# Four engines' written-out stage orders replaced in a fused four-layer kernel, loop and both ends

## The reference, cut to what matters

```python
# layer 0: attention (16 query heads, 1 key/value head, band mask), gate, RMS norm, minus the mean over tokens
attn = softmax(mask(q @ k.T * scale)) @ v @ Wo + bo
gate = silu(concat([attn, x]) @ Wg + bg)
out = rms(attn * gate + x * (1 - gate)) * w;  x = out - mean(out, over tokens)
# layer 1: each token attends to 3 context rows near its index, weights relu(score)^2 / sum
x = x + near_attention(rms(x), rms(ctx)) @ Wo
# layer 2: self attention, then cross attention, 16 heads of 64, layer norms, relative position bias
x = attention(ln(x), ln(x)) + x;  x = attention(ln(x), ln(ctx)) + x
# layer 3: a Mamba-2 block (4-tap causal conv, 8 heads, gated, RMS norm), then cross attention, 8 heads of 32
x = x + rms(scan(silu(conv(rms(x) @ Win))) * silu(z)) @ Wout
x = x + softmax(mask(ln(x) @ Wq @ k.T)) @ v @ Wo
```

## Time and profile before

| | |
|---|---|
| timed runs | 1283.28, 1285.97, 1286.2 us (median 1285.97) |
| span of the profiled execution | 1284.9 us (its only time on record), mean granted TensorE clock 0.985 |
| head: start to the loop's first stage | 237.93 us |
| loop: 11 turns | 809.48 us, 73.59 each |
| tail: last turn's end to the last instruction | 237.49 us |
| busy share of PE, DVE, ACT, POOL | 95%, 69%, 60%, 26% |

### The profile page before, as it was taken

The page is one execution under the profiler, slowest core; times in us unless marked ns, Lnnn a source line. Parts: engine busy times, 40 slices in busy tenths (PEclk is TensorE's granted clock), DMA queues, the critical chain, the costliest instruction groups (busy, mean ns, idle before and its releaser), DMA issues.

```text
span 1284.9 us, 27988 instructions
## 1 busy us (share of the span) xinstructions
PE 1225.8 (95%) x9644; PEld 988.3 (77%) x9644; DVE 883.1 (69%) x3414; ACT 770.2 (60%) x2658; POOL 332.6 (26%) x750
## 2 busy tenths in 40 slices
PE   5899899999999999999999999999999999999887
PEld 3568687788788787788788788878878787788665
DVE  4674667687686768678686867768676876836464
ACT  3447457565766756576775757576575655655533
POOL 2111441312314141222314131231414123112150
PEclk9899899999999999999999999999999999999899
DMA  7730001001010100001010100101010010000000
GB/s 219 290 120 13 34 2 43 13 11 44 0 49 4 49 4 25 28 8 45 0 49 4 44 9 8 45 0 49 4 49 4 16 37 34 5 6 1 9 1 13
DMA packets 28620, 44.67 MB, mean 35 GB/s; under 512 B 4716, under 2 KB 20620, under 8 KB 28056
## 3 DMA queue, kind: packets, MB, share of 16 engines
q1 hardware_dynamic: 26264, 31.42, 7.4%
q0 software_dynamic: 2304, 12.58, 2.7%
HBM read 37.64 MB, written 6.35 MB: 34 GB/s over the span
## 4 chain that ended last, share of the span: by engine, by line
PE 89%; DVE 5%; ACT 2%; issue 1%; DMA 1%; POOL 1%; SPq 0%; DVEq 0%; POOLq 0%
PE psum L574 57%; PE psum L568 11%; PE psum L759 5%; PE psum L782 4%; PE psum L625 3%; PE psum L821 2%; PE psum L876 1%; PE psum L836 1%; PE psum L647 1%; PE psum L916 1%; PE psum L677 1%; ACT A L938 1%; PE psum L891 1%; DVE A L1175 1%; ACT A L930 0%
## 5 line engine op out<-in xcount | busy, mean ns | idle before, releaser
L938 ACT ACTIVATE A<-A,small_ 128x128 f32<-128x128 f32 x640 | 248.5, 396 | 49.6 <-DVE small_ L1175 49.6
L930 ACT ACTIVATE A<-psum 128x512 f32<-128x512 f32 (+2 forms) x231 | 155.7, 700 | 173.7 <-PE psum L568 152.9
L568 PE MATMUL psum<-cst,A 128*128 128x128 f32 x888 | 131.5, 281 | 20.8 <-DVE A L1287 6.9
L568 PEld LDWEIGHTS psum<-cst,A 128*128 128x128 f32 x888 | 101.9, 143 | 43.8 <-issue 14.5
L938 ACT ACTIVATION_READ_ACCUMULATOR A<-A,small_ 128x1 f32 x640 | 125.0, 195 | 0.0
L1501 POOL TENSOR_SCALAR small_<-small_ 128x1 f32<-128x1 f32 x96 | 22.6, 236 | 370.1 <-DVE small_ L1189 203.7
L1175 DVE CUSTOM_DVE_ANT_0 A<-psum,cst 128x128 f32<-128x128 f32 x256 | 56.7, 287 | 66.6 <-PE psum L625 66.4
L1175 DVE CUSTOM_DVE_ANT_0 A<-psum,bias 128x128 f32<-128x128 f32 x264 | 58.4, 287 | 63.3 <-PE psum L759 63.3
L1185 DVE TENSOR_TENSOR A<-A,small_ 128x1024 f32<-128x1024 f32 x80 | 98.3, 1229 | 2.7
L938 ACT ACTIVATE sa_p<-sa_p,small_ 128x128 f32<-128x128 f32 x248 | 96.1, 398 | 4.3 <-DVE small_ L1175 4.3
L1366 DVE SCALAR_TENSOR_TENSOR A<-psum,half_cw,A 128x127 f32<-128x127 f32 (+2 forms) x270 | 70.7, 344 | 32.0 <-ACT A L1062 32.0
(11 more groups left out here) (314 smaller groups left out, 2886.8 us busy)
## 6 DMA issues: line engine op xcount, KB each, us to landing
kv_rows<-A SPq DMA_DIRECT2D x16, 256.0 KB
IN<-in_tokT SPq DMA_DIRECT2D x15, 256.0 KB, 2.6
A<-bias_rows SPq DMA_DIRECT2D x1, 2048.0 KB, 10.0
Wsakv<-in_wsa_kv SPq DMA_DIRECT2D x1, 2048.0 KB, 11.6
Wcakv<-in_wca_kv SPq DMA_DIRECT2D x1, 2048.0 KB, 12.8
ctx_end<-in_tokT SPq DMA_DIRECT2D x16, 128.0 KB, 2.2
out<-x_out SPq DMA_DIRECT2D x16, 128.0 KB, 1.7
IN<-in_ctx SPq DMA_DIRECT2D x15, 128.0 KB, 2.0
```

Source lines behind the costliest of these rows:

```text
L568: mm = pe.transpose(out[:, c * P:(c + 1) * P], src[:, c * P:(c + 1) * P], ident)
L930: return act.activation(out, in_, ACT.Copy)
L938: ins = act.activation(p[:, h * T:(h + 1) * T], p[:, h * T:(h + 1) * T], ACT.Exp, scale=-1.0, bias=sm(part, "nm", w * HU + h, w * HU + h + 1),
```

## The change

All twelve strings are replaced by other permutations (the same stages, each batch's part in the same inner order). In the loop, PE's `l0_s0`, `ca_v`, `ca_hat`, `ca_q`, `ca_s0` and both `sa_s` stages come earlier, `m_dtz`, `m_xbc`, `m_seg`, `m_heads`, `q3` later; between `m_xh` and `turn1` PE's new order is `l0_p1 sa_s0 l0_m1 m_heads kv1 attn0 sa_s1 ca_p0 gate0 ca_p1 m_sq m_out kv3 back0 ca_m hat3 sa_p0 center0 q3`, and DVE's from `m_xh` on is `m_xh sa_s0 m_heads ca_p1 attn0 m_sum sa_s1 sa_p0 m_sq gate0 m_out kv3 hat3 back0 sa_p1 center0 q3 turn1`. In the head, `o:bias_rows` and `o:l0_s0` come before `b:kv0` on PE; around batch 2's `near` stages (key `e`) `center0`, `turn1`, `near_q`, `sa_out` and `ca_out` come earlier than they did against `turn_o1`. At the tail's start `ca_q` moves ahead of `d:l0_m0`; at its end `h:hat3`, `h:c3_s`, DVE's `h:c3_p` and PE's `h:c3_out` each move ahead of the stage of batch 15 that they stood behind.

Two edits of code go with it. `m_tap` keeps its step marks per part (part 4 of two batches can now interleave): where another chained step of DVE came between two taps, the tap waits for all chained steps so far, otherwise per block as before. And the layer norm of the last attention gets small columns of its own, `r3` and `t3`.

```diff
@@ -117,25 +117,25 @@
 ORDER = {
-    "PE": "3132414314323141323412431112144432143421421312421414",
-    "Activation": "344341324314141323123114123142231422414",
-    "DVE": "21124134114443423134343142414442241214141112314",
-    "Pool": "4322411441112",
+    "PE": "3131324134343212314241214112313444134214142132421414",
+    "Activation": "334343142431124134211241313214213242414",
+    "DVE": "23121411431342443431424314224144412141411413124",
+    "Pool": "2124413144112",
 }
 
 
 HEAD = {
-    "PE": "obooobobooboooobobobobooooboooobooobeeabbeabaaebaebeaecdeddadacdaedacecdcdeccdecececdecegigfihfgifghgihgifighfgifiihfffihgifgffhgihiihfhifif",
...
-    "DVE": "oobooboobobbboooooooooobooooobooeaeabebbeaebbbeabddadaaddedacdeccecceceeeedecihifhgifiifhgffigfggfgffifhffifhhffihiifiiigihf",
...
+    "PE": "ooobobooooboooboobboobbbooooooboooobeebaebabaaeabebeaedeeddcadcadadacecdcdcecedececdccegegfifhigfighighgifghfihfiiigfffigfhfighfigihihfhifif",
...
+    "DVE": "oooboboobobbobooooooooobooooobooeaebaebbeaebbbeabddadaaddaceddeccecececedeecefhiihgfiiihffgfgfiggfffhfigfffihhfihfiifigiihif",
...
 }
 
 TAIL = {
-    "PE": "bdbadadbdabdcddddbdbacadbcdacdbacbdabacdbadacgaggagcfgacgfcafeifgfegfefgigfeieifieifeeeieeeifieieeihhjjhjhhjhjjhhhjjjhhjhjjhjhjhj",
...
-    "DVE": "cddbcadadddaaadbbadcabdbdaabdacddadaaccdggacagbaggcgfaegfefeeffegefieieeieeeeieieifeehijhjhhhjhjjhjhjhjhjhjhhjjjhhjjhjhj",
...
+    "PE": "bdbadadbabcdbddbdddadbacdcadcbdacadcbabddabagcagggcafgcagacffegfefgefigfgiefieifiefieeeieeeifieieeihhjjhjhhjhjjhhhjjhjhhjjjhjhhjj",
...
+    "DVE": "ddcadbcdaddabaadabdbcadbadbaadcadddaacdgcgaagcabggacefggeffeefeffegieieeieeeeieieiefehijhjhhhjhjjhjhjhhjhjhhjjhjjhjhjjhj",
...
 }
 
 
@@ -334,7 +334,7 @@
 
         _soft = [("nm", 2 * HU), ("sm", 2 * HU), ("rc", 2 * HU)]
         _norm = [("bn", 6), ("mv", 2), ("r", 1), ("r1", 1), ("ssq", 1), ("ssq1", 1), ("t1", 2)]
-        _mamba = [(n, HM) for n in ("dtp", "ab", "u", "den", "s", "sq", "po", "dt", "a")]
+        _mamba = [(n, HM) for n in ("dtp", "ab", "u", "den", "s", "sq", "po", "dt", "a")] + [("r3", 1), ("t3", 1)]
         _near = [("ms", 2), ("cr", 2), ("w", NEAR * H1), ("dn", H1)]
         small_places = {
             1: _soft + _norm + _near,
@@ -1351,7 +1351,7 @@
                 need(t, "m_thz")
                 dve.scalar_tensor_tensor(m.sz, m.thz, 1.0, m.Pd, ALU.add, ALU.mult).then_inc(sem["m_sz"], 1)
 
-            taken = [0] * CC
+            taken = {}
 
             def m_tap(d):
 
@@ -1359,17 +1359,23 @@
                     m = W4(t)
                     if d == 1:
                         need(t, "m_acc")
+                        taken[m.part] = [0] * CC, 0
+                    mine, reached = taken[m.part]
+                    beside = steps[0] == reached
+                    if d > 1 and not beside:
+                        after(steps[0])
                     for c in range(CC):
-                        if d > 1:
-                            after(taken[c])
+                        if d > 1 and beside:
+                            after(mine[c])
                         to = m.acc[:, c * T + d:(c + 1) * T]
                         ins = dve.scalar_tensor_tensor(to, m.P_4[:, c * T:(c + 1) * T - d],
                                                        half_cw[:, c * TAPS + TAPS - 1 - d:c * TAPS + TAPS - d],
                                                        to, ALU.mult, ALU.add)
                         if d < TAPS - 1:
-                            taken[c] = step(ins)
+                            mine[c] = step(ins)
                     if d == TAPS - 1:
                         ins.then_inc(sem["m_conv"], 1)
+                    taken[m.part] = mine, steps[0]
                 return run
 
             def m_silu(t):
@@ -1429,7 +1435,7 @@
             def normed3(t):
                 m = W4(t)
                 need(t, "c3_rstd")
-                normed(m.part, m.x5[:], m.hat3, sm(m.part, "r"), "c3_hat")
+                normed(m.part, m.x5[:], m.hat3, sm(m.part, "r3"), "c3_hat")
 
             def query3(t):
                 m = W4(t)
@@ -1495,9 +1501,9 @@
                 steps[0] += 1
                 pool.wait_ge(sem["pool_chain"], steps[0])
 
-            def rsqrt(part, out, src, scale, eps, name):
-
-                t = sm(part, "t1", 0, 1)
+            def rsqrt(part, out, src, scale, eps, name, at="t1"):
+
+                t = sm(part, at, 0, 1)
                 then(pool.tensor_scalar(t, src, scale, eps, ALU.mult, ALU.add))
                 pool.tensor_tensor(out, t, neg_half[:, 0:1], ALU.pow).then_inc(sem[name], 1)
 
@@ -1617,7 +1623,7 @@
             def deviation3(t):
                 m = W4(t)
                 need(t, "c3_var")
-                rsqrt(m.part, sm(m.part, "r"), sm(m.part, "mv", 1, 2), 1.0, 1e-5, "c3_rstd")
+                rsqrt(m.part, sm(m.part, "r3"), sm(m.part, "mv", 1, 2), 1.0, 1e-5, "c3_rstd", "t3")
 
             stages = {
                 "inputs": [ctx_rstd], "attn0": [near_rows], "gather": [gather], "back0": [rms0], "center0": [rms1],
```

More of the change, by code:

```diff
@@ L119 @@
 ORDER = {
-    "PE": "3132414314323141323412431112144432143421421312421414",
-    "Activation": "344341324314141323123114123142231422414",
-    "DVE": "21124134114443423134343142414442241214141112314",
-    "Pool": "4322411441112",
+    "PE": "3131324134343212314241214112313444134214142132421414",
+    "Activation": "334343142431124134211241313214213242414",
+    "DVE": "23121411431342443431424314224144412141411413124",
+    "Pool": "2124413144112",
 }
 HEAD = {
-    "PE": "obooobobooboooobobobobooooboooobooobeeabbeabaaebaebeaecdeddadacdaedacecdcdeccdecececdecegigfihfgifghgihgifighfgifiihfffihgifgffhgihiihfhifif",
-    "Activation": "oooboobobobobobbobobaeebaaebeedaecadadeacaddccededcceccdcefgfgifghgfiifhigfighgifihigfighhfhihfif",
-    "DVE": "oobooboobobbboooooooooobooooobooeaeabebbeaebbbeabddadaaddedacdeccecceceeeedecihifhgifiifhgffigfggfgffifhffifhhffihiifiiigihf",
-    "Pool": "oooboobobbaaebedadceeexdgfhifhffiiiih",
+    "PE": "ooobobooooboooboobboobbbooooooboooobeebaebabaaeabebeaedeeddcadcadadacecdcdcecedececdccegegfifhigfighighgifghfihfiiigfffigfhfighfigihihfhifif",
+    "Activation": "oooooboobobbbobbobobaebeaaebeeedaadcadeaacddcceddecccdeccegffgfhigfgiifhigfhigifihgifgihghfihhfif",
+    "DVE": "oooboboobobbobooooooooobooooobooeaebaebbeaebbbeabddadaaddaceddeccecececedeecefhiihgfiiihffgfgfiggfffhfigfffihhfihfiifigiihif",
+    "Pool": "obooooobbebaeabdadeecexdfihfifhgfiiih",
 }
 TAIL = {
-    "PE": "bdbadadbdabdcddddbdbacadbcdacdbacbdabacdbadacgaggagcfgacgfcafeifgfegfefgigfeieifieifeeeieeeifieieeihhjjhjhhjhjjhhhjjjhhjhjjhjhjhj",
-    "Activation": "baabadbdddaddbdadcabdcbacbdbcbdacgagcagcafgcfegfefigegefgfifeeiifeifeieiieiehhjhjjhjhhjjhjhjhjhjhj",
-    "DVE": "cddbcadadddaaadbbadcabdbdaabdacddadaaccdggacagbaggcgfaegfefeeffegefieieeieeeeieieifeehijhjhhhjhjjhjhjhjhjhjhhjjjhhjjhjhj",
-    "Pool": "cdabdacdddaagcegfegeeihjhjhjhj",
+    "PE": "bdbadadbabcdbddbdddadbacdcadcbdacadcbabddabagcagggcafgcagacffegfefgefigfgiefieifiefieeeieeeifieieeihhjjhjhhjhjjhhhjjhjhhjjjhjhhjj",
+    "Activation": "baabdabdbaddddcadadbbdcdacbcbdbacgagcgcafacgegffefgegeigffeifeiifeieifeiieiehhjjhjhjhhjjhjhjhjhhjj",
+    "DVE": "ddcadbcdaddabaadabdbcadbadbaadcadddaacdgcgaagcabggacefggeffeefeffegieieeieeeeieieiefehijhjhhhjhjjhjhjhhjhjhhjjhjjhjhjjhj",
+    "Pool": "acdadddcbdaagecgfegeehijhjhhjj",
 }
```

## The result

The changed kernel takes 1272.07 us at the median of four runs (1268.93 to 1272.87) against 1285.76 (1283.28 to 1286.2), a ratio of 0.9891 with a 95% interval of 0.9876 to 0.9906: 1.1% faster, 13.7 us. The forecast was 1273.

A forecast was written before the change was run, and what follows sets the result against it. The prediction took PE to bound the loop, with VectorE bounding the new m_xh-to-turn1 stretch, and more to win in the ends. Its terms, -1 - 3.5 - 4 - 4 - 2.5 + 0.8 + 1.2 = -13, gave 1273 us, range 1265 to 1283.

The forecast's parts named there:

- Loop, -1: Loop, m_xh to turn1: VectorE bounds the new stretch at 20.2 us, so -0.07 a turn, -1 us over 11 turns.
- the floor of 19.6: Loop, m_xh to turn1: 19.6 us of work for PE if no producer were late.
- rival (1): Loop: VectorE keeps up and PE gets its 0.67 a turn, -6.4 us more, 1266.6; chance 0.15.
- Head, start, -3.5: Head's start: o:l0_s0 no longer stands behind b:kv0's wait for tokens and starts about 14.3; -3.5 us (0 to -5.2).
- Head, middle, -4: Head, around batch 2's turn_o1: earlier center0, turn1, near_q, with ca_out already behind turn_o1; -4 us (0 to -6).
- Tail, start, -4: Tail's start: ca_q before l0_m0 and ca_s0 before l0_m1 cover batch 15's wait for ScalarE; -4 us (0 to -6).
- Tail, end, -2.5: Tail's end: earlier batch 14 stages, and a shorter store wait (-0.5) at the last addition; -2.5 us (+0.5 to -3.5).
- The rest, +0.8 and +1.2: Head's four extra shape switches, +0.8 us; waits coming back one stage later in windows not followed at both ends, +1.2.
- Code edits, 0: The edits of m_tap and the small columns add no instruction and cost 0.
- (2): Head and tail give only half, their long chains binding one stage later: -14 becomes -7, 1280; chance 0.18.
- (4): Whole kernel: the strings only move waits about and nothing comes of them, 1286; chance 0.08.
- rival (3): Loop: back0's power queued behind m_out's on GpSimd delays VectorE, center0 and turn1 every turn; up to +16.5, 1289.5; chance 0.09.

The follow-up runs named there:

- e_joint: Changed kernel with l0_m0 moved behind m_seg in the loop on PE and ScalarE, adding a change of array shape: 1275.34 us, turn 73.59.
- e_start: Old orders with the new code, only b:kv0 moved behind o:l0_s0 in PE's head order: 1281.64 us, ratio 0.9969 to the kernel before.
- e_end: Changed kernel with batch 15's minima ahead of batch 14's multiply on VectorE and seven of nine spare matmuls ahead of h:c3_p: 1271.55 us, ratio 0.9891 to before.
- e_code: Kernel before with the code edits alone, all old stage orders: 1284.79 us, ratio 1.0006 to before.
- e_head: Kernel before with the new head order alone, old loop and tail orders, new code: 1275.81 us, ratio 0.9937 to before.
- e_tail: Kernel before with the new tail order alone, old loop and head orders, new code: 1277.3 us, ratio 0.9947 to before.
- e_pool: Changed kernel with one more unread one-column power on GpSimd behind that of m_out, every turn: 1276.68 us, turn 73.87.
- after_again: A second profile and timing of the unedited changed kernel: 1270.24 us, ratio 0.9883 to the kernel before.

## Why the prediction was right, and where it was not

The sign, the size and the places were right, but several terms missed and cancel: that 1273 and 1272.07 agree within 1 us is partly luck. The loop, the windows that I hadn't followed and the end of the tail gave more than their terms, the head's two less. In the order of the prediction:

- **Loop, -1: measured -2.2** in the first profile, about -1.7 with the longer first turns. The step that failed is the sum of 20.2 for VectorE, from which PE was to stall at `hat3`, `center0` and `turn1`. PE's stretch from the end of `m_xh` to `turn1` takes 507.12 - 487.49 = 19.63: the floor of 19.6 (`l0_m1` comes 0.09 late behind `sa_s0`, as I feared), and none of the three stages named is late. VectorE was late by less because I gave `m_out`'s power the long time of the earlier trace rows; it takes 0.56, and with it went all but 0.15 of the 0.5 us wait at `back0`. So rival (1)'s premise was true in this stretch (-0.64 a turn), but 0.37 comes back right behind it, at `c3_s`, which I had put outside the stretch and not followed, and 0.07 at `c3_p`: -0.20. The floor's price of 0.2 for a change of shape is confirmed by e_joint.
- **Head, start, -3.5: measured -2.1** over all profiles, -2.3 in the one of e_start, 4.0 us (2.3 to 5.5) in its timed runs. `l0_s0` begins where the first constants let it, at 14.3 to 16.4, and I took 14.3. How much of the rest is lost in batch 0's chain up to `sa_q` is open.
- **Head, middle, -4: measured -3.3.** `turn_o1` came at 152.0 in a head that was some 4 us ahead by then, and `ca_ctx` follows 0.42 behind it, as forecast.
- **Tail, start, -4: measured -4.2**, free of the low clock that followed.
- **Tail, end, -2.5: measured -2.6**, but not as worked out. The store's wait cost 1.4, not 0.5: the time behind PE's last matmul fell from 4.0 to 2.6. `h:c3_p` comes earlier and `j:c3_p` with it, while batch 15's minima now stand behind batch 14's multiply, where 1.4 us lay that e_end took (with the spare matmuls moved too).
- **The rest, +0.8 and +1.2: measured -0.7 in the head and -0.4 in the tail.** Waits do come back (+1.8 between `a:m_heads` and `f:ca_q`), but other windows that I hadn't followed give more. I also missed that a spare matmul stands between the two `c3_m` of the old tail, so that its changes of shape fall from 55 to 53.
- **Code edits, 0:** e_code.

The measured terms sum to -15.6 in profiles (-15.1 with the first turn's mean), against 13.7 and 15.7 us in the two timed comparisons. Rivals (2) and (4) fall with e_head and e_tail; rival (3) was not met, but e_pool shows its mechanism, and the longer first turns are GpSimd delaying VectorE too. One sign named for the forecast did not show: `hat3` and `turn1` released by VectorE. Neither is, but for the first turn of after_again, where they wait 0.66 and 0.37 us.

## What to carry to other kernels

In a loop of back-to-back PE stages, an engine with 27% idle time can still hold the turn through one unbroken row of its work: look for producer ends within 0.1 us of PE's starts, since a wait of zero is printed nowhere and yet is the bound. Before you fill a hole in PE, ask what the stage behind the hole feeds, and what that chain meets next. In pipelined ends, compare stretches between named stages over several profiles; the scatter of the whole (here some 5 us) sits in a few of them.

## What the runs showed of the hardware

**A GpSimd power beside a VectorE operation with two SBUF inputs is longer only if it starts second.** In the kernel before, in all eleven turns, the power starts 0.02 to 0.03 us after such an operation. GpSimd, then VectorE:

```profile
510.06 1.07 POOL L1502 TENSOR_TENSOR small_<-small_,neg_half 128x1 f32<-128x1 f32 x1
```

```profile
510.04 0.69 DVE L1424 TENSOR_TENSOR A<-A,cst 128x512 f32<-128x512 f32 x1
```

In the changed kernel the same two meet in the loop, but the power starts first (502.99), VectorE's operation at 503.10:

```profile
503.10 0.69 DVE L1430 TENSOR_TENSOR A<-A,cst 128x512 f32<-128x512 f32 x1
```

Both take their plain time, 0.56 and 0.69. e_code, with the old order and the new code, has the eleven long ones again (1.07 to 1.08). This is the rule of the Trainium skill that I held against the change ("GPSIMD Engine Reference", section "1. Specifications": SBUF interfaces shared with VectorE, contention with instructions of two SBUF inputs). The traces agree that the two contend, but not that a denser VectorE makes powers longer: an order of starts 0.1 us apart decides. The 14 profiles hold 206 meetings of a power with this operation. In 123 the power starts first, by 0.03 us or more, and takes 0.54 to 0.58. In 83 it starts second: 0.02 to 0.03 behind it takes 1.07 to 1.09, 0.07 to 0.08 behind 1.03 to 1.04, 0.13 behind 0.97 to 0.98, 0.4 behind (e_pool's added one) 0.69 to 0.70. Each of the 83 ends 1.10 to 1.11 after the start of VectorE's operation, which is twice 0.55. I read it so: the second stands still until some 0.55 of the other has passed, and then takes its plain time. VectorE's operation takes 0.69 or 0.70 in all 206, so in this pair it loses nothing, first or second.

**One change of array shape costs 0.20 us** (e_joint): 0.09 in the whole-array stage ahead of it, 0.11 in the one behind. The rule of "TensorEngine Tiling (Array Packing)" in the Trainium skill, section "Key Properties" (a change of mode drains TensorE), is agreed with: joining two partial stages saves one change, not both.
